# Second attention pass of batch b run together with the first pass of batch b+1, in 16-slot stretches on two rings of single PSUM banks

## The reference, cut to what matters

```python
h = attention16(x)                      # softmax(q k / 4) v, 16 heads of 16
h = concatenate([h, txt], axis=1)       # 589 tokens
u = layernorm(h)
xp = u @ x_proj.T                       # 64 low-rank columns, 16 B, 16 C
delta = softplus(xp[..., :64] @ dt_proj.T + b)
for t: state = exp(delta_t * A) * state + delta_t * B_t * u_t ; y_t = sum(state * C_t)
h = h + y + u * D_skip
h = h + one_expert_of_14(layernorm(h))
h = h + causal_attention(layernorm(h))
h = h + two_experts_of_128(layernorm(h))
```

## Time and profile before

| what | us |
|---|---|
| median of 3 runs (lowest, highest) | 1209.46 (1206.95, 1211.32) |
| span of the profiled execution | 1222.6 |
| busy in it: PE, DVE, ACT, POOL | 929.1, 763.9, 440.4, 205.3 |

### The profile page before, as it was taken

The page is one execution under the profiler, slowest core; times in us unless marked ns, Lnnn a source line. Parts: engine busy times, 40 slices in busy tenths (PEclk is TensorE's granted clock), DMA queues, the critical chain, the costliest instruction groups (busy, mean ns, idle before and its releaser), DMA issues.

```text
span 1222.6 us, 14392 instructions
## 1 busy us (share of the span) xinstructions
PE 929.1 (76%) x4656; PEld 511.5 (42%) x4657; DVE 763.9 (62%) x1348; ACT 440.4 (36%) x819; POOL 205.3 (17%) x248
## 2 busy tenths in 40 slices
PE   6898989879888688974286529999588887548880
PEld 2323432334323243222253229998356565324440
DVE  4803589996899968999779931111467756732225
ACT  1174138750287501873352203444123331212220
POOL 1000001110011100111000142333000203355550
PEclk9989798976889858796687859999799998769995
DMA  3199206873058730597656436664501400249926
GB/s 100 27 326 330 84 23 160 212 166 100 18 151 206 172 109 1 135 213 159 160 181 211 148 128 192 196 195 149 233 1 46 179 6 14 75 140 398 402 75 253
DMA packets 75259, 185.57 MB, mean 152 GB/s; under 512 B 12010, under 2 KB 48573, under 8 KB 72512
## 3 DMA queue, kind: packets, MB, share of 16 engines
q1 hardware_dynamic: 60800, 148.11, 36.9%
q0 software_dynamic: 14400, 36.71, 13.7%
HBM read 124.88 MB, written 43.69 MB: 138 GB/s over the span
## 4 chain that ended last, share of the span: by engine, by line
PE 35%; DVE 29%; issue 19%; DMA 9%; POOL 3%; ACT 2%; another core or an unknown queue 1%; SPq 1%; POOLq 0%; DVEq 0%; ACTq 0%
DVE hst L1639 8%; PE ps L646 7%; DVE hC L1649 5%; PE ps L1139 5%; DMA bc<-bc_dram 4%; DVE mxn L1588 4%; PE ps L1015 3%; PE ps L623 3%; PE ps L1127 2%; POOL ys_dram L1546 2%; PE ps L1087 2%; DMA yodd<-hC 2%; PE ps L741 2%; DVE Hs L2170 1%; PE ps L633 1%
## 5 line engine op out<-in xcount | busy, mean ns | idle before, releaser
L1588 DVE TENSOR_REDUCE mxn<-ps 128x2 f32<-128x1024 f32 x128 | 150.6, 1220 | 60.3 <-PE ps L646 60.0
L1639 DVE TENSOR_TENSOR_SCAN hst<-dA,dBu 128x1180 f32<-128x1180 f32 x64 | 166.9, 2608 | 3.1 <-ACT dA L1209 2.6
L646 PE MATMUL ps<-Kh,Qh 32*128 32x512 f32 x512 | 122.6, 763 | 25.4 <-DVE mxn L1588 24.6
L1217 ACT ACTIVATE Ph<-ps 128x1024 f32<-128x1024 f32 x128 | 125.2, 1077 | 24.1 <-PE ps L741 23.5
L741 PE MATMUL ps<-Qh,Kh 32*128 32x512 f32 x512 | 111.0, 717 | 5.6 <-ACT Ph L1217 5.4
L1630 DVE TENSOR_TENSOR dBu<-dtu,bc 128x1180 f32<-128x1180 f32 x64 | 88.0, 1380 | 14.7 <-DMA bc<-bc_dram 14.5
L1649 DVE TENSOR_TENSOR hC<-hst,bc 128x1180 f32<-128x1180 f32 x64 | 87.2, 1362 | 9.6 <-DMA yodd<-hC 9.6
L1525 POOL DMA_DIRECT2D yS<-hC x24 | 20.8, 868 | 426.6 <-DVE hC L1649 426.6
L1139 PE MATMUL ps<-ring,xgT 128*64 128x256 f32 x512 | 70.1, 395 | 13.6 <-ACT xgT L1477 9.4
L1906 DVE TENSOR_TENSOR yo<-ps,b2r 128x256 f32<-128x256 f32 x32 | 13.6, 425 | 106.4 <-PE ps L938 106.4
L754 PE MATMUL ps<-Ph,Vh 128*32 128x512 f32 x512 | 73.7, 649 | 7.1 <-ACT OT L1221 4.4
(11 more groups left out here) (263 smaller groups left out, 1443.8 us busy)
## 6 DMA issues: line engine op xcount, KB each, us to landing
bc<-bc_dram SPq DMA_DIRECT2D x64, 590.0 KB, 5.9
ring<-in_we SPq DMA_DIRECT2D x16, 2048.0 KB
W<-in_w SPq DMA_DIRECT2D x46, 512.0 KB, 5.9
yS<-hC POOLq DMA_DIRECT2D x24, 590.0 KB, 7.9
yodd<-hC POOLq DMA_DIRECT2D x24, 590.0 KB, 7.8
xs_dram<-zeros SPq DMA_DIRECT2D x1, 8224.0 KB, 43.8
xg<-xs_dram SPq DMA_DIRECT2D x16, 514.0 KB
ys_dram<-zeros SPq DMA_DIRECT2D x1, 5120.0 KB, 48.3
```

Of the source, the lines that this page charges most:

```text
L646: m = nc.tensor.matmul(ps[:, banks.start + hh % 2, :], Qh[HR * hh:HR * (hh + 1), hg, P * i:P * (i + 1)], Kh[HR * hh:HR * (hh + 1), hg, :], ...
L1217: nc.scalar.activation(Ph[:, n % 2, 2 * g:2 * g + 2, :], ps[:, turned_banks(2 * n + g), :], ACT.Exp, scale=float(HD) ** -0.5).then_inc(act ...
L1588: nc.vector.tensor_reduce(slots32(mxn[:, hg % 2, i, :])[:, 2 * g:2 * g + 2, HD], ps[:, score_banks(b, 2 * (QT * hg + i) + g), :], AX.X, AL ...
L1639: nc.vector.tensor_tensor_scan(hst[:, k % 2, :, :].rearrange("p c t -> p (c t)"), dA[:, k % 2, :, :].rearrange("p c t -> p (c t)"), dBu[:, ...
```

## The change

The order becomes, on each engine:

1. `first_maxima`: units 0 to 9 of batch 0's first pass (pairs of banks, three sets), and all its projections of Q and K.
2. `attend_ahead(eb)` for eb = 0, 1, 2: a stretch of 16 slots. Slot n holds the second pass's unit n of batch eb and one unit of a first pass: the last 6 of eb in slots 0 to 5, the first 10 of eb+1 in slots 6 to 15 (for eb = 1 the last 6 had already been done, and slots 0 to 5 have none). PE alternates by head: one score matmul, one turned matmul, with the heads of the second in the order 2, 3, 0, 1; then the weighted sum of slot n-1. The scores go round a ring of three single banks (5, 6, 7), the turned scores round another (0, 1, 2), bank 3 holds the weighted sum, bank 4 projections and turned maxima. The stretch also has 6 projections of Q or K of eb+1 (slots 4, 5, 8, 9, 12, 13) and 4 turns of maxima.
3. Between the stretches: `first_chain` (the chain of batch 0 with the last 6 units of batch 1's first pass), `scan_beside_chain(0)`, `scan_beside_chain(1)` (the scan of cb with the chain of cb+1 beside it, no attention; in the second `turn_both(0)` and its `add_y`).
4. `scan_beside_attention`: the scan of batch 2 with units 10 to 15 of batch 3's first pass (4 in step 0, 2 in step 1), its whole second pass (spread as before) and its chain. `last_scan` is the scan of batch 3.

DVE now reduces one bank at a time in the stretches, and ACT takes one bank at a time. `uT` is kept for two batches, `dBu` has 2 buffers in place of 3. The skip term of batches 0 to 2 is no longer put into `yS` by ACT: `turn_both` adds it as a third matmul for each piece, in three rounds of at most two token tiles; POOL's first DMA into `yS` is a plain copy, and waits until `turn_both` of the batch before is done.

```diff
-        SETS = (0, 2, 5)
...
+        FIRST_SETS = ((0, 1), (2, 3), (5, 6))
+        A_RING, B_RING = (5, 6, 7), (0, 1, 2)
+        PV, MISC = 3, 4
+        LAG = 6
+        ALONE = NU - LAG
+        TURNED = (2, 3, 0, 1)
+        Y_ROUNDS = ((0, 2), (2, 4), (4, 5))
...
+        def unit_at(eb, n):
+            return (eb, ALONE + n) if n < LAG else (eb + 1, n - LAG)
+
+        def remaining(n):
+            return range(min(NU, ALONE + 4 * n), min(NU, ALONE + 4 * n + 4))
...
+            def score_head(b, u, h):
...
+                if freed_by(k):
+                    pe.wait_ge(dve_max, freed_by(k))
+                return nc.tensor.matmul(ps[:, score_bank(k), :], Qh[HR * h:HR * (h + 1), hg, P * i:P * (i + 1)],
+                                        Kh[HR * h:HR * (h + 1), hg, :], start=True, stop=True)
...
+            def turned_head(b, n, x):
...
+                if k >= len(B_RING):
+                    pe.wait_ge(act_p, k - len(B_RING) + 1)
+                nc.tensor.matmul(ps[:, B_RING[k % 3], :], Kh[HR * h:HR * (h + 1), hg, P * j:P * (j + 1)],
+                                 Qh[HR * h:HR * (h + 1), hg, :], start=True, stop=True).then_inc(pe_st, 1)
...
+            def both(b, u, eb, n):
+                for x in range(4):
+                    if u is not None:
+                        score_one(b, u, x)
+                    if n is not None:
+                        turned_head(eb, n, x)
+                if n:
+                    weighted(eb, n - 1)
...
+            def attend_ahead(eb):
+                ab = eb + 1
+                for n in range(NU):
+                    if n == 2:
+                        turn_maxima(eb, 2)
+                    elif n in (4, 8, 12):
+                        project(ab, n // 4 - 1, 0)
+                    elif n in (5, 9, 13):
+                        project(ab, n // 4 - 1, 1)
+                    elif n == 6:
+                        turn_maxima(eb, 3)
+                    elif n in (10, 14):
+                        turn_maxima(ab, n // 4 - 2)
+                    elif eb == 0 and n < 2:
+                        project_v(0, n)
+                    b, u = unit_at(eb, n)
+                    both(b, None if eb == 1 and n < LAG else u, eb, n)
+                weighted(eb, NU - 1)
...
+            def scan_beside_chain(cb):
+                eb, ab = cb + 1, cb + 2
+                project(ab, 3, 0)
+                project(ab, 3, 1)
+                turn_heads(eb, range(HG))
+                project_v(ab, 0)
+                project_v(ab, 1)
+                turn_values(eb, 0)
+                turn_values(eb, 1)
+                if cb:
+                    for r in range(len(Y_ROUNDS)):
+                        turn_both(cb - 1, r)
+                project_out(eb, 0)
+                project_out(eb, 1)
+                turn_tokens(eb)
+                project_x(eb)
+                project_dt(eb)
+
+            def scan_beside_attention():
+                cb, eb = NB - 2, NB - 1
                 for n in range(NS):
+                    if n == 1:
+                        turn_maxima(eb, 2)
+                    elif n == 2:
+                        turn_maxima(eb, 3)
+                    ahead = remaining(n)
+                    behind = units_ahead(n)
+                    for k in range(max(len(ahead), len(behind))):
+                        both(eb, ahead[k] if k < len(ahead) else None, eb, behind[k] if k < len(behind) else None)
+                    if n == 1:
+                        for r in range(len(Y_ROUNDS)):
+                            turn_both(cb - 1, r)
...
-                if n == 0:
-                    pool.wait_ge(act_ys, b + 1)
+                if n < 2 and b:
+                    pool.wait_ge(pe_yt, y_count(b - 1, 2))
```

More of the change, by code:

```diff
@@ L602, in _, with project @@
         def _(pe):
-            def project(b, hg, which, bank):
+            def project(b, hg, which):
+                bank = which if b == 0 and hg == 0 else MISC
                 if hg == 0 and which == 0:
@@ L807, in turn_both @@
                     rows = P if i < QT else LP - S
+                    tokens = slice(P * i, P * i + rows)
                     for c in range(KC):
[L809 to L812 removed]
@@ L1146, in two_experts @@
                     multiply(j)
-            front(0, None)
-            back(0, None)
-            for b in range(NB - 1):
-                front(b + 1, b)
-                back_ahead(b + 1, b)
-            back(None, NB - 1)
+            first_maxima()
+            attend_ahead(0)
+            first_chain()
+            attend_ahead(1)
+            scan_beside_chain(0)
+            attend_ahead(2)
+            scan_beside_chain(1)
+            scan_beside_attention()
+            last_scan()
             one_expert()
@@ L1160, in _, with take_q @@
         def _(act):
-            def take_q(b, hg, which, bank):
+            def take_q(b, hg, which):
+                bank = which if b == 0 and hg == 0 else MISC
                 act.wait_ge(pe_q, 2 * (HG * b + hg) + which + 1)
@@ L1703, in back_ahead, with unit_maxima, first_maxima @@
-            def back_ahead(eb, cb):
-                drive(cb, 0)
+            def unit_maxima(b, u):
+                maxima_turned(b, u)
+                for h in range(4):
+                    head_maxima(b, u, h)
+            def first_maxima():
+                for u in range(ALONE):
+                    maxima_turned(0, u)
+                    pair_maxima(0, u, 0)
+                    pair_maxima(0, u, 1)
+                    if u % QT == 0 and u:
+                        minus(0, u // QT - 1)
@@ new lines, in attend_ahead, with first_chain @@
+            def attend_ahead(eb):
+                ab = eb + 1
+                for n in range(NU):
+                    b, u = unit_at(eb, n)
+                    if not (eb == 1 and n < LAG):
+                        unit_maxima(b, u)
+                    if n == 2:
+                        minus(eb, 2)
+                    elif n == 6:
+                        minus(eb, 3)
+                    elif n in (10, 14):
+                        minus(ab, n // 4 - 2)
+            def first_chain():
+                unit_maxima(1, ALONE)
+                values(0)
+                unit_maxima(1, ALONE + 1)
+                unit_maxima(1, ALONE + 2)
+                residual(0)
+                moments(0)
+                unit_maxima(1, ALONE + 3)
+                scales(0)
+                unit_maxima(1, ALONE + 4)
+                unit_maxima(1, ALONE + 5)
+                step_size(0)
+                input_size(0)
+                drive(0, 0)
```

730 lines of the change are left out of this document (383 added, 347 removed).

## The result

The median went from 1210.39 us (4 runs, 1206.95 to 1214.40) to 1332.16 us (4 runs, 1326.65 to 1336.06): a ratio of 1.0994, 95% interval 1.0940 to 1.1049, or 121.8 us slower. The profiled execution after has a span of 1330.1, 2.1 under its median. That of before was 12.2 over the median of these runs, so the spans differ by 107.5 only.

What follows compares the result with a forecast made beforehand. The limit changes by stage: DVE in scans covering second passes, PE in first passes from batch 2 on. Stages built from 3.93 us slots summed to +79 on 1222.6, scaled to +78, 1288 us; forecast 1250 to 1320, range 1215 to 1345.

Steps and rivals of the forecast that it cites:

- rival of the lower clock: A third of the 48 stretch slots at 1.2 GHz, 7.1 each: 51 us more, 1338; chance 0.12.
- The sign of being wrong: Profile signs against the forecast: slots near 3.1 or below, clock 0.50 inside stretches, scan much under 90, early `values` of batch 3.
- first chain: Between stretches 0 and 1: chain work, six units at DVE's 0.61 a bank (14.6) and ACT's copies (5.5), 43.9 in all.
- scan of batch 0: After stretch 1: 91.6 as before, as DVE bounded it, plus 2.8 for step size and input size: 94.4.
- scan of batch 2: PE's attention delays `values` by 42, to 96.4, including 5.6 for decays ahead of exponentials; stage 139.
- The slot: In a stretch, the ring of three makes s3 await s0's bank and t1 await ACT's exponential: 3.93 us, between 3.13 and 7.1.
- Nothing is saved by PE's absence: In the scan of batch 0, losing the second pass beside it does not shorten the 91.6, which DVE set.
- A slot without a score costs the same: Stretch 1's first six slots have the same wait for t2's exponential, so also cost 3.93 each.
- The yS wait: Scan of batch 1: POOL's first DMA into `yS` stands behind `turn_both(0)`, delaying DVE's step 2; cost 8, bounds 0 and 12.
- scaling by the 1.1%: Whole kernel: median taken as 1.1% under the profiled span, so +79 on 1222.6 became +78, 1288 us.
- The rival of the closed gaps: Stretches: s3 and t1 do not hold back the weighted sum, slot 3.13, +15 to +29, 1224 to 1238; chance 0.19.
- The faster rival: Slot falls to DVE's and ACT's 2.6, a stretch to 57: -16, 1193; break-even slot 2.9; chance 0.07.

Runs made afterwards that it cites:

- Experiments 1 to 4: Kernel after: stretch 2's scores thinned, 1337.67; batch 2's turned scores thinned, 1318.84; score ring of two banks, 1371.83; six turned-score banks where no scores run, 1282.55.
- experiment 9: Kernel before with the second passes of batches 1 and 2 run ahead of the scans, not beside them: 1264.46 beside 1193.20, ratio 1.0575.
- experiment 1: Kernel after with stretch 2's score matmuls and reductions over 16 of 512 columns: 1337.67 us, single run.
- experiment 5: Kernel after with six units of batch 1's first pass moved from the first chain into slots 0 to 5 of stretch 1: 1309.03 us, ratio 1.0730.
- experiment 4: Kernel after with six banks for turned scores in 18 slots without scores, in stretch 1 and the scan of batch 2: 1282.55 us, ratio 1.0599.
- experiment 8: Kernel before with five unread matmuls on PE ahead of the first passes of batches 2 and 3: 1216.11 us, ratio 1.0040.
- experiment 10: Kernel before with a third set of two banks for the first eleven score pairs of batches 2 and 3: 1182.37 beside 1193.20, ratio 0.9905.
- experiment 7: Kernel after with four unread matmuls on PE between the chain of batch 0 and stretch 1: 1325.57 us, ratio 1.0928.

## Why the prediction was right, and where its sum fell short

The forecast, slower through a slot of 3.9 and an uncovered second pass, held. The time was 44 above it and inside the range, but outside the 1250 to 1320 that had been given 0.58, and next to the 1338 of the rival of the lower clock. The sign of being wrong that the prediction named, a clock of 0.50 inside stretches, is there in one of three. Stage by stage, each in the profiled execution, with stretch 1 counted from PE's first matmul at 178.80:

| stage | foretold | measured | difference |
|---|---|---|---|
| opening | 48.8 | 47.4 | -1.4 |
| stretch 0 | 82.4 | 79.6 | -2.8 |
| first chain | 43.9 | 51.8 | +7.9 |
| stretch 1 | 78.4 | 91.1 | +12.7 |
| scan of batch 0 | 94.4 | 102.5 | +8.1 |
| stretch 2 | 78.4 | 75.6 | -2.8 |
| scan of batch 1 | 106.6 | 105.2 | -1.4 |
| scan of batch 2 | 139.0 | 151.8 | +12.8 |

- **The slot** was foretold at 3.93 by the wait of a ring of three and measured 3.96; the reduction of one bank, taken as 0.68 between 0.61 and 1.22, is 0.686, the exponential, taken as 0.65, is 0.596. Experiments 1 to 4 show the mechanism: less work leaves it, one bank less gives 4.55, three more let another engine set it. Two of three stretches came within 3 us.
- **"Nothing is saved by PE's absence"** in the scans is right, and experiment 9 gives the loss of cover a price by itself: 71, beside the 122 in all.
- **"A slot without a score costs the same"** is the step that failed. It is true of the wait inside such a slot, and leaves out the clock and what ACT still had to do when the stretch began. PE's timeline in stretch 1, such slots at either level:

```profile
178.80 2.08 PE L749 MATMUL ps<-Qh,Kh 32*128 32x512 f32 x6 [2.82 <-issue]
184.58 5.37 PE L749 MATMUL ps<-Qh,Kh 32*128 32x512 f32 x10 [3.71 <-ACT Ph L1299]
...
192.79 2.08 PE L749 MATMUL ps<-Qh,Kh 32*128 32x512 f32 x6
195.61 2.07 PE L749 MATMUL ps<-Qh,Kh 32*128 32x512 f32 x2 [0.73 <-ACT Ph L1299]
...
199.47 2.08 PE L749 MATMUL ps<-Qh,Kh 32*128 32x512 f32 x6
...
217.10 1.14 PE L749 MATMUL ps<-Qh,Kh 32*128 32x512 f32 x6
218.97 1.12 PE L749 MATMUL ps<-Qh,Kh 32*128 32x512 f32 x2 [0.73 <-ACT Ph L1299]
```

  The wait is 0.73 at either level. At the lower one the matmuls take twice as long, so a slot is 199.47 - 192.79 = 6.68. Slots 0 to 3, a turn and a projection take 30.8, from 178.80 to 209.62; the sum has 17.4 for them (slot 0 has no weighted sum). Some 3.9 of the difference lie ahead of 184.58: ACT's last softplus step and the scan's first decay, from 179.95 to 183.96, stand before the first exponentials, and PE waits 3.71. The other 9.5 are the clock. Together that is all of stretch 1's 12.7.
- **The scan of batch 2**: the same slots without scores. ACT's timeline shows them, and DVE's what they held up.

```profile
638.91 1.57 ACT L1299 ACTIVATE Ph<-ps 128x512 f32<-128x512 f32 x3 [1.43 <-PE ps L749]
...
652.27 1.57 ACT L1299 ACTIVATE Ph<-ps 128x512 f32<-128x512 f32 x3 [3.33 <-PE ps L749]
```

```profile
643.70 2.62 DVE L1738 TENSOR_TENSOR_SCAN hst<-dA,dBu 128x1180 f32<-128x1180 f32 x1 [7.72 <-ACT dA L1291]
...
657.06 2.62 DVE L1738 TENSOR_TENSOR_SCAN hst<-dA,dBu 128x1180 f32<-128x1180 f32 x1 [8.17 <-ACT dA L1291]
...
662.99 0.57 DVE L1757 RECIPROCAL rsum<-ps 128x32 f32<-128x32 f32 x2 [3.31 <-PE ps L786]
```

  Four slots and the last sum cost some 11 more than at the full clock, and `values` comes at 109.8 in the stage, not 96.4. The decays, which stand behind exponentials on ACT, now hold DVE up by about 8, twice. Foretold was 5.6 for decays ahead of exponentials; the other way round, exponentials ahead of decays, was left out.
- **The rival of the lower clock**, with a chance of 0.12, named this cost and not its place. It asked for a third of 48 slots at 7.1. Eight slots ran through at 0.50 (6.7 each in the scan of batch 2), all of them without scores, and the stretches with both rings had 1.00 and, right behind a scan, 0.97.

  In stretch 0 the two rings leave PE no gap (busy 79.58 of 79.60), because where one ring's matmul waits the other's still streams, and the clock stays at 1.00. Without scores the 0.73 in each slot stands open. Stretch 1 was entered at 0.50 behind 2.82 idle, and stayed there to 209; in the scan of batch 2 the clock fell to 0.50 in the middle of such slots, at about 629.

  The rule cited from the Trainium skill (TensorE: Matmul & The Clock Gate, A second HAM failure mode: psum-queue depth-cycling) speaks of small idle times between groups of matmuls while PE cycles through banks. The trace agrees with it in part for the slots without scores, which had both levels with the same 0.73, and not for a full stretch, where the prediction had weighed it: cycling alone did not bring the clock down. Nor is a gap in each slot enough by itself: with thin scores the slots of experiment 1 had one of 0.53 and ran at 0.94 from 395 to 455.
- **The yS wait** was foretold at 8 between 0 and 12 and measured 3.07. Its row, with the one of scan 0 that was not foretold:

```profile
368.37 1.39 DVE L1748 TENSOR_TENSOR hC<-hst,bc 128x1180 f32<-128x1180 f32 x1 [3.74 <-DMA yodd<-hC]
...
474.10 1.39 DVE L1748 TENSOR_TENSOR hC<-hst,bc 128x1180 f32<-128x1180 f32 x1 [3.07 <-DMA yS<-hC]
```

- **The scan of batch 0** took 8.1 over the sum: besides this yodd wait, one of 2.00 for a decay and five of 0.67 to 1.55 for the broadcasts of B and C. Why those DMAs came later than before wasn't tried.
- **The first chain** took 7.9 more, at a clock of 0.80. Without the six units, in experiment 5, it takes 31.3, where the sum less their 14.6 has 29.3. So, by these two executions, some 5.9 of the 7.9 lie in the units, taken at DVE's 0.61 a bank alone, and 2.0 in the rest.
- **Rest.** Behind the changed part the profile has 625.1 for 630.2, not foretold. And scaling by the 1.1% that the profile of before lay over its median was wrong for a profile that lies 2.1 under its own: of the 44 that the forecast was short, 33 are stages, 5 go off for the rest, and 16 are this.

**The rival of the closed gaps** asked for a slot of 3.13; no slot with scores came under 3.9. **The faster rival** asked for under 2.9; only slots with six banks and no scores had some (2.1 in stretch 1 of experiment 4, 193.17 to 195.25), and even there the kernel stayed 6% slower than before.

## What to carry to other kernels

Before work is moved away from beside a stage, ask what that stage waits for: PE's second passes under scans that DVE filled were free, and two of them laid open alone cost 71 us. Two passes on one engine overlap only as far as their buffers let them, and the period of a slot is worked out in advance from when a bank comes free: matmul, evacuation, next matmul, counted round the ring. Try the longer ring alone first; on the kernel before it gave 11 us without any reordering.

## What was not expected of the hardware

- TensorE at 0.50 is not a sign that it has nothing to do. In experiment 8 it was busy 23.03 of 24.0 in such a window, in experiment 10 23.29 of 26.0.
- Slots with turned scores alone ran at either level with the same gap of 0.73: at 0.50 from 178.6 to 209.0, at full speed at 217.1. Four or five matmuls of filling ahead gave the full clock to the first slot's six records in one kernel and to the first unit in the other, and right behind them it was the lower one.
- The clock differed between executions in the same slots: the last slots of the scan of batch 2 took 6.7 in the profile after and 3.9 in that of experiment 7, whose edit lies elsewhere. The spread of that kernel's runs is 1312.81 to 1333.18. What decides it stayed open.
- Taking work from PE made a stage longer: in experiment 1 stretch 2 took 84.5 for 75.6, with the clock at 0.51 over its first 25.4 us. In the kernel after PE's matmuls there were back to their short durations 4 us into the stretch (376.6). That the thinner scores kept the clock down isn't shown by itself.
